# A row of softmax reciprocals made before, not after, the value products in an attention kernel

## What is computed

```
q = ((x @ Wq_c.T + bq_c) @ Wq_up.T + bq_up)            # 32 heads of 128 + 64
kv_nope, kv_rope = split(x @ Wkv_c.T + bkv_c, 64)
k_nope, v = split(kv_nope @ Wkv_up.T + bkv_up, 128)    # per head
attn = softmax(q @ [k_nope, kv_rope].T / sqrt(192))
out = (attn @ v) @ Wo.T + bo                           # Wo 512 x 128, summed over the heads
```

## Time and profile before

| | us |
|---|---|
| median of three executions | 1855.05 |
| the profiled execution, its time | 1852.05 |
| its span, first to last instruction | 1850.2 |
| mean granted clock of TensorE | 0.994 |

### The profile page before, as it was taken

One profiled execution on the slowest core, in us unless ns is written; L12 is line 12 of the kernel. 1 busy time (PEld: TensorE's weight loads), 2 busy tenths in 40 slices (PEclk: granted clock), 3 DMA queues, 4 the chain that ended last, 5 costly groups with the idle time before them and its releaser, 6 DMA issues. The chain is left out here.

```text
span 1850.2 us, 23339 instructions
## 1 busy us (share of the span) xinstructions
PE 1650.0 (89%) x7316; PEld 753.7 (41%) x7316; DVE 1618.4 (87%) x2088; ACT 1416.3 (77%) x1979; POOL 969.6 (52%) x1355
## 2 busy tenths in 40 slices
PE   7988988998989889889989898898898988988799
PEld 6733333333333333333333333333333333333344
DVE  6679999999989999999989999999989999999565
ACT  5578888888878888888878888888878888888422
POOL 3246556565555565565555655555546555555320
PEclk9999999999999999999999999999999999999999
DMA  6599999999999999999999999999999999999611
GB/s 211 179 188 191 187 190 186 188 190 183 190 173 185 186 190 188 190 183 191 183 176 190 186 188 190 183 190 183 188 175 189 188 189 185 190 187 182 150 44 48
DMA packets 1092405, 330.84 MB, mean 179 GB/s; under 512 B 1070336, under 2 KB 1076768, under 8 KB 1092288
## 3 DMA queue, kind: packets, MB, share of 16 engines
q1 hardware_dynamic: 1080128, 296.22, 87.1%
q0 software_dynamic: 12160, 33.18, 6.6%
HBM read 50.39 MB, written 10.49 MB: 33 GB/s over the span
## 5 line engine op out<-in xcount | busy, mean ns | idle before, releaser
L969 DVE TENSOR_REDUCE mx<-S 128x1 f32<-128x1024 f32 x512 | 621.1, 1213 | 123.9 <-PE S L830 123.9
L925 ACT ACTIVATE S<-S,shift,unscale 128x1024 f32<-128x1024 f32 x512 | 602.0, 1176 | 158.0 <-DVE shift L975 145.9
L961 DVE TENSOR_TENSOR halves<-S,halves 128x1024 f16<-128x1024 f32 x512 | 621.6, 1214 | 2.6 <-ACT halves L934 2.6
L934 ACT ACTIVATE halves<-S 128x1024 f16<-128x1024 f32 x512 | 523.8, 1023 | 16.1
L828 PE MATMUL S<-kvTH,qeH 128*128 128x512 f16 x1024 | 392.2, 383 | 97.6 <-POOL qeL L740 93.2
L753 POOL TENSOR_TENSOR diagonal<-ident,recip 128x512 f32<-128x512 f32 x128 | 131.7, 1029 | 493.0 <-PE O L862 480.1
L830 PE MATMUL S<-kvTH,qeL 128*128 128x512 f16 x1024 | 388.1, 379 | 0.0
L829 PE MATMUL S<-kvTL,qeH 128*128 128x512 f16 x1024 | 388.1, 379 | 0.0
L840 PE MATMUL O<-PT,kvn 128*128 128x512 f16 x1024 | 243.6, 381 | 0.0
L975 DVE SCALAR_TENSOR_TENSOR shift<-mx,unscale,c_lift 128x1 f32<-128x1 f32 x512 | 225.8, 441 | 18.2
L828 PEld LDWEIGHTS S<-kvTH,qeH 128*128 128x128 f16 x1024 | 99.4, 97 | 332.1 <-POOL qeL L740 146.9
(11 more groups left out here) (263 smaller groups left out, 2018.6 us busy)
## 6 DMA issues: line engine op xcount, KB each, us to landing
weff<-weff_scratch POOLq DMA_DIRECT2D x126, 192.0 KB, 4.6
wv<-in_wv POOLq DMA_DIRECT2D x128, 64.0 KB, 3.1
PT<-halves SPq DMA_TRANSPOSE x512, 5.0
raw<-in_raw SPq DMA_DIRECT2D x8, 772.0 KB, 6.7
weff_scratch<-w_split SPq DMA_DIRECT2D x8, 768.0 KB, 5.2
x<-in_x SPq DMA_DIRECT2D x4, 1024.0 KB, 6.8
x_all<-in_x SPq DMA_DIRECT2D x3, 1024.0 KB, 5.6
out<-y SPq DMA_DIRECT2D x3, 1024.0 KB, 4.3
```

Source lines behind the costliest of these rows:

```text
L925: nc.scalar.activation(S[:, t % SLOTS, :], S[:, t % SLOTS, :], ACT.Exp, bias=shift[:, col:col + 1], scale=keep["unscale"][:, 0:1], accum_o ...
L934: nc.scalar.activation(halves[u][:, 0, :], S[:, t % SLOTS, :], ACT.Copy).then_inc(high_out, 1)
L961: v.tensor_tensor(halves[u][:, 1, :], S[:, t % SLOTS, :], halves[u][:, 0, :], ALU.subtract).then_inc(low_out, 1)
L969: v.reduce_max(mx[:, col:col + 1], S[:, t % SLOTS, :], AX.X).then_inc(max_ready, 1)
```

## The change

The two reciprocal rows get SBUF tiles of their own (`recip_row0`, `recip_row1`), and `osum` goes. TensorE repeats the row of group g - 1 in body g, behind scores(2), before that group's value products in body g + 1. ScalarE copies this row to SBUF ahead of exp(3) and no longer copies the sum. VectorE multiplies the sum, where it stands in `O`, by the copied row. `next_queries` moves from behind scores(2) to behind scores(1). The line on GpSimd that waits for `row_filled` is not edited; what it waits for is now filled one body earlier.

```diff
 def values():
-    if on:
-        pe.wait_ge(q_copied, g + 1)
+    if g >= 3:
+        pe.wait_ge(onorm_ready, g - 2)
+    pe.wait_ge(row_out, g - 1)
...
-def repeat_row(out):
-    pe.wait_ge(diagonal_ready, g - 1)
+def repeat_row(k, out):
+    pe.wait_ge(ones_set, 3)
+    pe.wait_ge(diagonal_ready, k + 1)
     mm(out, square[:], diagonal[:].rearrange("p u c -> p (u c)"), start=True, stop=True).then_inc(row_filled, 1)
...
-if g == NG + 1:
-    repeat_row(S[:, 2, 0:BLK])
 if exists(g - 2):
     values()
 if g == NG:
-    pe.wait_ge(ones_set, 3)
-    repeat_row(S[:, 2, BLK:2 * BLK])
+    repeat_row(g - 1, S[:, 2, 0:BLK])
 if on:
     scores(1)
-    if g >= 2:
-        pe.wait_ge(ones_set, 3)
-        pe.wait_ge(o_out, g - 1)
-        repeat_row(O[:])
-    scores(2)
     if exists(g + 1):
         next_queries()
+    scores(2)
+    if exists(g - 1):
+        if exists(g + 1):
+            pe.wait_ge(q_copied, g + 2)
+        elif g >= 2:
+            pe.wait_ge(onorm_ready, g - 1)
+        repeat_row(g - 1, O[:])
...
 # ScalarE
-if exists(g - 2):
-    if g >= 3:
-        act.wait_ge(onorm_ready, g - 2)
-    act.wait_ge(pv_done, g - 1)
-    nc.scalar.activation(osum[:], O[:], ACT.Copy).then_inc(o_out, 1)
+def copy_row(out):
+    act.wait_ge(row_filled, g)
+    if g >= 3:
+        act.wait_ge(onorm_ready, g - 2)
+    nc.scalar.activation(row[1 - par][:], out, ACT.Copy).then_inc(row_out, 1)
 if exists(g):
     for u in range(UN):
         if u == 2 and exists(g + 1):
             copy_q(g + 1, (h + 1) % NH, 1 - par)
+        if u == 3 and exists(g - 1):
+            copy_row(O[:])
         exp(u)
         high(u)
 if g == NG:
+    copy_row(S[:, 2, 0:BLK])
...
 # VectorE
-def normalized(row):
-    dve.wait_ge(o_out, g - 1)
-    dve.wait_ge(row_filled, g - 1)
+def normalized():
+    dve.wait_ge(pv_done, g - 1)
+    dve.wait_ge(row_out, g - 1)
     if g >= 3:
         dve.wait_ge(onorm_low, g - 2)
-    v.tensor_tensor(onorm[:], osum[:], row, ALU.mult).then_inc(onorm_ready, 1)
+    v.tensor_tensor(onorm[:], O[:], row[par][:], ALU.mult).then_inc(onorm_ready, 1)
```

More of the change, by code:

```diff
@@ L620, in attention @@
         wvs = sb("wv_scaled", [KVL, VH])
-        onorm, onormH, onormL, osum = (keep[n] for n in ("onorm", "onormH", "onormL", "osum"))
+        onorm, onormH, onormL = (keep[n] for n in ("onorm", "onormH", "onormL"))
+        row = [sb(f"recip_row{i}", [P, BLK]) for i in range(2)]
         diagonal, square = sb("diagonal", [P, UN, P]), sb("ones_square", [P, P])
@@ L637, in attention @@
                  "wv_split", "onorm_high", "onorm_low", "ffn_in", "row_ready", "bo_added", "projected0", "summed0",
-                 "stats0", "std0_done", "rstd0_done", "sign_ready", "q_filled", "q_high", "q_copied", "q_low", "o_out")
+                 "stats0", "std0_done", "rstd0_done", "sign_ready", "q_filled", "q_high", "q_copied", "q_low", "row_out")
         (bv_in, ones_set, scores_ready, max_ready, shift_ready, probs_ready, high_out, low_out,
@@ L641, in attention @@
          wv_split, onorm_high, onorm_low, ffn_in, row_ready, bo_added, projected0, summed0,
-         stats0, std0_done, rstd0_done, sign_ready, q_filled, q_high, q_copied, q_low, o_out) = (sem(n) for n in names)
+         stats0, std0_done, rstd0_done, sign_ready, q_filled, q_high, q_copied, q_low, row_out) = (sem(n) for n in names)
         ident = keep["ident"]
@@ L1022, in body @@
                         if u == 1 and g >= 2:
-                            normalized(O[:])
+                            normalized()
                         if UN * g + u:
@@ L1039, in body @@
                     reciprocals()
-                    normalized(S[:, 2, BLK:2 * BLK])
+                    normalized()
                     add_projection(UN - 1)
@@ L1053, in body @@
                 if g == NG + 1:
-                    normalized(S[:, 2, 0:BLK])
+                    normalized()
                     dve.wait_ge(wv_done, NG - 1)
@@ L1288, in layer @@
             "sign": sb("sign", [P, 2]), "factor": sb("factor", [P, 1]), "xn2": sb("xn2", [P, UN, HID]),
-            "osum": sb("osum", [P, BLK]), "onorm": sb("onorm", [P, BLK]),
+            "onorm": sb("onorm", [P, BLK]),
             "onormH": sb("onormH", [P, BLK], F32R), "onormL": sb("onormL", [KVL, BLK], F32R),
```

## The result

The changed kernel takes 2039.32 us (median of four executions) against 1854.88 of the kernel before: a ratio of 1.0987, with a 95% interval of 1.0954 to 1.1021. It is slower by 184 us; forecast were 1984 and a range of 1940 to 2050. The profiled execution took 2039.29 us.

A forecast was written before the change was run, and what follows sets the result against it. The prediction took a circle of waits, 12.67 us a body, as the bound. A body of 13.71 us gave 125 x 1.04 = 130; 1852.05 + 130 - 1 = 1981, plus 3.00 for the median: 1984 us, range 1940 to 2050.

The forecast's parts named there:

- The sum's own upper bound: Whole kernel: 14.26 us a body, +199, 2053 us, if (b) fails and `shift` keeps its 0.77.
- the clock's rival: TensorE's clock falls at the new stall: 2030 us if in a third of the bodies, 2123 in all; chance 0.12.
- sign of being wrong: Profile: projection stall below 1.6, granted clock below 0.98, or period under 13.4 would show the forecast wrong.
- (a): TensorE before the projection: its wait for `onorm` loses 2.17 us of cover; TensorE stands 2.33 us.
- (b): VectorE's `shift` of unit 1: `diagonal` is gone before it, so it falls from 0.77 to 0.22, -0.55 us.
- (c): TensorE before the next scores(0): projection, `copy_q` and `qeL` come earlier, closing the 0.89 us wait.
- (d): ScalarE still makes one copy of 0.60 us, now the row; VectorE's product stays at 0.67 us.
- (e): New waits: repeated row for `copy_q`, hidden by some 0.1 us; value products for the copied row, 0.31 us.
- The sum of a body: Loop period after the change: 5.99 + 2.80 + 3.64 + 1.28 = 13.71 us, +1.04 a body.
- The price of one fall: TensorE at the lower clock: each fall costs at least 1.11 us, from eight value products taking 3.00 against 1.89.
- The rival with `diagonal` unmoved: GpSimd reaches `diagonal` late, behind `wv` work, and its collision with `shift` remains: 2053 us; chance 0.05.
- the one in which scores(2) passes the projection: TensorE's queue: the projection's wait does not stop scores(2), leaving (b) alone, -69, 1786 us; chance 0.02.

The follow-up runs named there:

- e2: The changed kernel with the projection put back behind scores(2) and the repeated row behind scores(3); 1788.4 us, ratio 0.9626.
- e3: The kernel before with one edit, the projection moved ahead of scores(2); 2054.3 us, ratio 1.1065.
- e4: e1 with GpSimd's `diagonal` held until the fourth spare matmul ends, which puts its collision with `shift` back; 2054.3 us, ratio 1.1052.
- e10: The kernel before with two buffers for `diagonal`, so that GpSimd need not wait for the repeated row of the same body; 1787.3 us, ratio 0.9611.
- e5: e1 with ScalarE's copy of the row ahead of exp(2) instead of exp(3); 1946.1 us, ratio 1.0489.
- e1: The changed kernel with eight spare matmuls, results overwritten, between scores(1) and the projection; 1982.1 us, ratio 1.0671.
- e6: The changed kernel with VectorE's `onorm` moved ahead of the maximum of scores(1); 2097.8 us, ratio 1.1287.
- e9: The changed kernel with `onorm` ahead of the maximum of scores(1), the row's copy ahead of exp(2) and `copy_q` ahead of exp(1); 1778.1 us, ratio 0.9579.

## Why the prediction was right, and where it fell short

The sign, the range and the mechanism of the longer body held. The forecast was 55 us low, nearly all of it by one term, the clock. That the time lies inside the range is in part luck. The sum's own upper bound, 2053, stood for a `shift` that keeps its 0.77, which did not happen, and the range reached the mild half of the clock's rival. By its own sign of being wrong, a granted clock below 0.98, the account without the clock failed: it was 0.964.

- (a), the uncovered stall: 2.33 computed, 2.33 measured. e2 and e3 show from both sides that it comes from the place of the projection.
- (b), `shift` from 0.77 to 0.22: as forecast, and e4 and e10 give it its price, 72 and 70 us (1857.5 - 1787.3).
- (c), the wait for `qeL`: gone, as forecast.
- (d), `onorm`: it reads PSUM and the SBUF row in 0.684 instead of 0.674, so the 0.67 stands.
- (e), the copied row: 0.31 forecast, 0.25 measured, 0.27 by e5.
- The sum of a body: 13.71 forecast, 13.74 measured. Two small misses offset each other. The copied row is 0.06 less late, and scores(3) with `output` takes 2.28 (1011.83 to 1014.11), not 2.20. The 0.23 for the last matmul was explained as 1.28 over five, which is 0.26, and it is 0.33 in this body (1013.78 to 1014.11).
- The step that failed is the clock, which the sum took at nothing and which stood as a rival with a chance of 0.12. It came in about a quarter of the bodies, the mild half of that rival (2030 computed). It is worth 57 us by e1, 54 of them in the loop. The price of one fall, at least 1.11 from eight value products, was too low: a long body is 1.5 longer, since the low clock reaches from scores(2) over the repeated row. The row chosen to weigh against it, a stall of 2.35 at the loop's head that kept the clock, was a single case, and the loop has 125 such stalls.
- The rival with `diagonal` unmoved did not come. Nor did the one in which scores(2) passes the projection: TensorE waited for `onorm` in 125 bodies.

The two parts add up in the profiled executions. Of the loop's 1800.1 - 1616.2 = 183.9 us, the longer body has 129.9 (e1_fill against the kernel before) and the clock 54.0 (the changed kernel against e1_fill). The stretch ahead of the loop is 3.4 longer, the one behind it the same, 107.7: together the 187.3 by which the spans differ, 2037.5 against 1850.2. What makes those 3.4 was not tested.

The Trainium skill, "SBUF — State Buffer", sections "Who interferes with whom" and "Summary: rules for kernel authors", has a VectorE instruction with two SBUF inputs wait for a GpSimd instruction that reads SBUF and started first, to its end. `shift` is such an instruction, and the traces here agree with three partners (`diagonal`, `onormL`, `qeL`): 0.50 to 1.15 in the rows shown instead of 0.22, each ending within 0.02 of its partner.

## What to carry to other kernels

Before moving work ahead of a wait, count what stood between producer and consumer on the waiting engine. It was the cover of the wait, and everything queued behind the moved work loses it.

A bank that passes from engine to engine needs all its hand-overs moved together, copy and product too, or the stall only moves one station on (e6 to e9).

A stall on TensorE that returns in every body has to be priced twice, once in time and once in clock: here 130 and 54 us. And a tiny VectorE instruction can take nearly as long as the GpSimd instruction that it meets: 1.15 beside one of 1.26.

## What was not expected of the hardware

A stall of 2.17 us in bodies of 13.74, beside one of 0.25, was enough for the clock to fall in about a quarter of the bodies, and the falls came in groups. Why some bodies of equal work have it and others not, no run here shows. Where the stall was 1.86 beside one of 0.67 (e3), the clock fell too, 31 times in the loop; with 0.87 (e2) it fell once. Eight matmuls whose results nobody reads, 1.7 us of work, made the kernel 57 us faster.
